# List pages padded ahead of time, y rows loaded two tiles at a time, and a memset behind every y scatter

## The reference

```python
x = x + xattn(layernorm(x), ctx, ctx, lens, Wq, Wk, Wv, Wo)   # keys past lens[b] are masked
u = layernorm(x)
s = softmax(u @ centroids.T + expert_biases)                  # 16 experts
topk_vals, topk_idx = top_k(s, 2)
routed = sum over the two of topk_vals * (u @ Wr[e].T + br[e])
shared = (u @ Ws[0].T + u @ Ws[1].T + bs[0] + bs[1]) / 2
x = x + u + routed + shared
```

## Time and profile before

| | us |
|---|---|
| Median of 3 runs (lowest, highest) | 261.77 (260.43, 262.01) |
| The profiled execution's own time | 261.29 |
| Its span in the profile | 259.4 |
| PE busy in the span | 219.6 (85%) |
| DVE busy | 152.5 (59%) |
| POOL busy | 106.3 (41%) |
| ACT busy | 95.1 (37%) |
| Mean granted TensorE clock, share of full | 0.953 |

### The profile page before, as it was taken

How to read it: one execution, slowest core, us unless ns; L and a number is a source line. 1 busy time by engine, 2 the same in 40 slices (tenths; PEclk the granted TensorE clock), 3 DMA queues, 4 the chain that set the end, 5 groups by cost and what they waited for, 6 DMA issues and landing times.

```text
span 259.4 us, 5036 instructions
## 1 busy us (share of the span) xinstructions
PE 219.6 (85%) x1530; PEld 184.8 (71%) x1530; DVE 152.5 (59%) x457; ACT 95.1 (37%) x241; POOL 106.3 (41%) x176
## 2 busy tenths in 40 slices
PE   7888999999999999999997943988669978576593
PEld 3767888888899998888875832867547757454482
DVE  1798778888888888888645930657503313140460
ACT  3114567566656666555442001222202213110022
POOL 1220222444444555444667200467566566574000
PEclk9999999999999999999999995999995999997689
DMA  6999990101011111100212693667455541200997
GB/s 170 361 247 373 426 414 16 43 20 44 20 44 41 43 41 44 42 22 27 79 39 71 159 206 100 201 197 221 137 169 163 172 130 36 90 17 9 332 382 248
DMA packets 20345, 36.30 MB, mean 140 GB/s; under 512 B 4059, under 2 KB 12765, under 8 KB 19936
## 3 DMA queue, kind: packets, MB, share of 16 engines
q1 hardware_dynamic: 13568, 22.50, 27.4%
q0 software_dynamic: 3792, 8.42, 9.2%
q10 hardware_dynamic: 2960, 5.07, 6.5%
HBM read 23.23 MB, written 14.71 MB: 146 GB/s over the span
## 4 chain that ended last, share of the span: by engine, by line
PE 67%; issue 9%; DMA 8%; DVE 4%; another core or an unknown queue 3%; SPq 3%; POOL 3%; ACT 1%; ACTq 1%; DVEq 0%; POOLq 0%
PE O L886 13%; PE T L808 7%; PE B L845 6%; PE B L953 5%; PE S L808 5%; PE A L808 4%; PE S L857 4%; PE B L1057 4%; PE T L1057 4%; PE A L1057 3%; DMA x<-in_x 3%; PE O L1057 3%; SPq L321 2%; PE S L1076 2%
## 5 line engine op out<-in xcount | busy, mean ns | idle before, releaser
L537 POOL DMA_INDIRECT lists<-urow,pos x32 | 32.8, 1024 | 41.6 <-PE S L857 34.0
L488 ACT ACTIVATE uTl<-S 128x256 f32<-128x256 f32 x47 | 17.0, 383 | 58.5 <-PE S L808 37.1
L415 ACT ACTIVATE pT<-T 128x512 f32<-128x512 f32 (+1 forms) x48 | 25.2, 526 | 30.4 <-PE T L808 28.7
L886 PEld LDWEIGHTS O<-vfront,pT 128*128 128x128 f32 x256 | 30.0, 192 | 0.1
L886 PE MATMUL O<-vfront,pT 128*128 128x34 f32 x256 | 29.9, 273 | 0.0
L665 DVE TENSOR_REDUCE rowmax<-S 128x16 f32<-128x1232 f32 x16 | 23.1, 1442 | 7.2 <-PE S L857 7.1
L568 POOL DMA_INDIRECT y<-yrow,padblock x16 | 15.8, 989 | 27.9 <-DVE yrow L786 20.7
L808 PE MATMUL T<-const,s_sb 128*128 128x128 f32 (+1 forms) x160 | 25.4, 273 | 2.0 <-DVE s_sb L680 1.2
L808 PEld LDWEIGHTS T<-const,s_sb 128*128 128x128 f32 (+1 forms) x160 | 19.1, 139 | 4.5 <-issue 2.7
L441 ACT ACTIVATE urow<-x,shift,rstds 128x256 f32<-128x256 f32 x32 | 19.1, 596 | 8.4 <-POOL shift L551 7.5
L680 DVE SCALAR_TENSOR_TENSOR s_sb<-S,rstds,scaledmax 128x1024 f32<-128x1024 f32 (+1 forms) x26 | 21.0, 850 | 0.0
(11 more groups left out here) (188 smaller groups left out, 432.7 us busy)
## 6 DMA issues: line engine op xcount, KB each, us to landing
padblock<-lists SPq DMA_DIRECT2D x32, 128.5 KB, 1.7
wr<-in_wrT SPq DMA_DIRECT2D x1, 4096.0 KB, 17.8
br<-in_br SPq DMA_DIRECT2D x1, 2048.0 KB, 21.9
wr<-y SPq DMA_DIRECT2D x8, 256.0 KB, 7.2
wr<-y ACTq DMA_DIRECT2D x8, 256.0 KB, 8.2
urow<-lists SPq DMA_DIRECT2D x15, 128.5 KB
xT<-in_xT SPq DMA_DIRECT2D x3, 512.0 KB, 7.7
x<-in_x SPq DMA_DIRECT2D x3, 512.0 KB, 8.0
```

What stands on the lines that cost most here:

```text
L415: nc.scalar.activation(pT[t % 2][0:rows, c0:c1, :], T[0:rows, 0:c1 - c0, :], ACT.Exp).then_inc(p_ready, 1)
L537: nc.gpsimd.indirect_dma_start(out=lists, out_offset=bass.IndirectOffsetOnAxis(ap=pos[:, t, c:c + 1], axis=0), in_=urow[t % NR][c][:, :], ...
L886: last = M(to, pT[t % 2][0:v.shape[0], c, :], v.rearrange("p h j -> p (h j)"), start=(c == 0), stop=(c == CH - 1), skip_group_check=True)
```

## The change

1. Padding. POOL's memset of padblock covers all 16 rows per partition instead of 4. SP fills the first three pages of every region at the start (filled), ahead of x and xT of tiles 8 to 15, which are now one load each (XGROUPS). Later pages are padded in the loop, three tiles ahead of any row that could reach them (REACH): seen becomes seen_runs, the tally eight times over (128 columns); PE multiplies it by one column of ones (count_runs), which gives each partition, an eighth of an expert, its expert's count; DVE rounds it to a page (reached, page), adds 4096 where the page is the same as a tile earlier (dropped), and so has the place in run_i; POOL writes 16 rows from each partition by an indirect DMA (pad_page), of which those past the bounds are dropped. pad_lists, padrow and the constant region go.
2. HANDOVER is 12, so the shared products of tiles 12 and 13 move behind the lists.
3. load_y takes two tiles, 512 KB; there are four loads on each queue.
4. POOL sets 256 columns of passed_x to zero behind every y scatter but the last.

```diff
-HANDOVER = 14
+HANDOVER = 12
+PARTS = P // EXPERTS
+RUN = P // PARTS
+REACH = 3
...
-        XGROUPS = [(0, 2), (2, 4), (4, 8), (8, 12), (12, 16)]
+        XGROUPS = [(0, 2), (2, 4), (4, 8), (8, 16)]
...
-            of = y_dram[b * SEQ * TOPK:(b + 1) * SEQ * TOPK, :].rearrange("(p t c) d -> t p c d", t=PER, c=TOPK)[t % PER]
-            eng.dma_start(ysum[:, t, :, :], of).then_inc(y_back[t], 16)
+            of = y_dram[b * SEQ * TOPK:(b + 1) * SEQ * TOPK, :].rearrange("(p t c) d -> p t c d", t=PER, c=TOPK)
+            eng.dma_start(ysum[:, t:t + 2, :, :], of[:, t % PER:t % PER + 2, :, :]).then_inc(y_back[t // 2], 16)
...
             sp.wait_ge(pool_set, 3)
-            sp.dma_start(lists[DUMMY:DUMMY + P, :], padblock[:, 0, :]).then_inc(padded, 16)
-            for g in (3, 4):
-                load_x(sp, g)
-                load_xT(sp, g)
+            sp.dma_start(lists[DUMMY:DUMMY + P, :], padblock[:, 0, :]).then_inc(filled, 16)
+            per_expert = lists[0:DUMMY, :].rearrange("(e n) w -> e n w", e=EXPERTS)
+            for page_of in range(REACH):
+                sp.dma_start(per_expert[:, page_of * P:(page_of + 1) * P, :].rearrange("e (b r) w -> e b (r w)", r=RUN),
+                             padblock[:, :, :].rearrange("p r w -> p (r w)")).then_inc(filled, 16)
+            load_x(sp, 3)
+            load_xT(sp, 3)
...
-            pad_lists(sp, mybir.EngineType.SP, 0, EXPERTS // 2)
-            sp.wait_ge(table_ready, 2)
+            sp.wait_ge(table_ready, 1)
...
-                    sp.wait_ge(padded, 16 + 16 * EXPERTS)
+                    sp.wait_ge(filled, 16 * (1 + REACH))
+                    for i in range(2):
+                        sp.wait_ge(padded[i], 16 * len(range(1 + i, TILES - REACH + 1, 2)))
...
-            pad_lists(act, mybir.EngineType.Activation, EXPERTS // 2, EXPERTS)
...
-            nc.gpsimd.memset(padblock[:, 0:PIECE, 0:D], 0.0)
+            nc.gpsimd.memset(padblock[:, :, 0:D], 0.0)
...
+                if t == 0:
+                    pool.wait_ge(filled, 16 * (1 + REACH))
+                if t >= REACH:
+                    pool.wait_ge(padded[(t - REACH) % 2], 16 * ((t - REACH) // 2 + 1))
...
+            def pad_page(t):
+
+                pool.wait_ge(run_ready, t)
+                nc.gpsimd.indirect_dma_start(
+                    out=runs, out_offset=bass.IndirectOffsetOnAxis(ap=run_i[:, t:t + 1], axis=0),
+                    in_=padblock[:, :, :].rearrange("p r w -> p (r w)"), in_offset=None,
+                    bounds_check=DUMMY // RUN - 1, oob_is_err=False).then_inc(padded[(t - 1) % 2], 16)
+
             for s in range(TILES + 3):
...
                 if is_tile(s - 3) and s != TILES:
                     scatter_rows(s - 3, s)
+                if 1 <= s - 3 <= TILES - REACH:
+                    pad_page(s - 3)
...
+                if k < LISTS - 1:
+                    if k >= 2:
+                        pool.wait_ge(paused, k - 1)
+                    nc.gpsimd.memset(passed_x[:, k % 2, :], 0.0).then_inc(paused, 1)
...
+                    opens = 1 <= t <= TILES - REACH
+                    if opens:
+                        V.tensor_scalar(reached[:, :], run_bank(t), REACH * P - FRONT - 0.5, 1.0 / RUN, ALU.add, ALU.mult
+                                        ).then_inc(reached_ready, 1)
...
-                        V.tensor_tensor(seen[:, :], seen[:, :], chosen[:, :], ALU.add)
+                        V.tensor_tensor(seen_runs[:, :, :], seen_runs[:, :, :],
+                                        chosen[:, :].unsqueeze(2).to_broadcast([P, EXPERTS, PARTS]), ALU.add)
...
+                    if opens:
+                        dve.wait_ge(reached_ready, t)
+                        link(V.tensor_scalar(page[:, t:t + 1], reached[:, :], EIGHTS, EIGHTS, ALU.add, ALU.subtract))
+                        link(V.tensor_scalar(dropped[:, :], page[:, t - 1:t], page[:, t:t + 1], BEYOND, ALU.is_equal, ALU.mult))
+                        V.scalar_tensor_tensor(out=run_i[:, t:t + 1], in0=page[:, t:t + 1], scalar=cst("run"), in1=dropped[:, :],
+                                               op0=ALU.add, op1=ALU.add).then_inc(run_ready, 1)
...
+            def count_runs(t):
+
+                if 1 <= t <= TILES - REACH:
+                    M(run_bank(t), seen_runs[:, :, :].rearrange("p e b -> p (e b)"), ones16[:, 0:1], start=True, stop=True)
...
-                pe.wait_ge(y_back[t], 16)
+                pe.wait_ge(y_back[t // 2], 16)
```

More of the change, by code:

```diff
@@ L182, in build @@
         start_i = sb("start_i", [LISTS, 1], i32)
-        padrow = sb("padrow", [1, EXPERTS], i32)
-        RUN, PIECE, NL, NY, NU = 16, 4, 24, 16, 4
+        reached = sb("reached", [P, 1])
+        page = sb("page", [P, TILES])
+        dropped = sb("dropped", [P, 1])
+        run_i = sb("run_i", [P, TILES], i32)
+        NL, NY, NU = 24, 16, 4
         padblock = sb("padblock", [P, RUN, ROW])
@@ L252, in build @@
         shifted_ready = sem("shifted_ready")
-        padded = sem("padded")
+        filled, padded, run_ready = sem("filled"), [sem(f"padded{i}") for i in range(2)], sem("run_ready")
+        reached_ready = sem("reached_ready")
+        paused = sem("paused")
         l_arrived = [sem(f"l_arrived{j}") for j in range(NL)]
```

52 lines of the change are left out of this document (25 added, 27 removed).

## The result

The changed kernel took 263.6 us in the median of 20 runs (260.7 to 268.2), the kernel before 260.8 us on the same chip. The ratio is 1.0067, with a 95% interval of 1.0042 to 1.0092: slower by 0.7%, within what I had called no change. The ratio leaves out executions more than 1.5% above the fastest of their kernel, seven of the twenty and the profiled one among them, and the medians of all lie 1.1% apart. I had said 264.9 us and 45% for slower by over 1%. The sum came out near the mark by luck: all that stands ahead of the list stage cost 5.8 us where I had said a gain of 3.2, and the list stage gained 2.4 us where I had said a loss of 5.3.

A forecast was written before the change was run, and what follows sets the result against it. TensorE was taken to bound the loop, with VectorE's add without slack, and GpSimd's scatters the lists. Minus 3.2, plus 5.3, plus 1.0 gave 264.4 us, and 0.5 for the median 264.9; range 255.0 to 269.5.

The forecast's parts named there:

- (f): List stage, memset behind 46 y scatters: interval 1.67 us against 1.29, stage 76.8 instead of 71.5, plus 5.3 us.
- (c): GpSimd in the loop, 13 more page DMAs: tile 12's page costs 1.26 us on the path, tile 13's nothing.
- (d): Start: padding memset grows to 3.8 us, then 6.4 MB of fill ahead of x and xT; cost nothing.
- (e): Before the lists: padding DMAs go, TensorE stays warm, first load to first y scatter 5.6 us; that scatter 3.2 earlier.
- (a): VectorE's page operations in the loop: 0.68 us ahead of each add, 6.8 us over ten periods.
- (b): TensorE in the loop: one more weight load and one-column product, 0.10 us per tile, hidden in its wait; nothing.
- the first rival: List stage: memset runs largely within the launch gap, interval near 1.45 us, stage 66.7, total 254.8; chance 0.22.
- (g): Two-tile y loads at the end: first result 1.3 us late, two more VectorE operations after the last arrival; plus 1.0 us.
- the other rivals: Free page operations, 259.4, chance 0.10; page scatters several times dearer, 270, 0.09; TensorE at 1.2 GHz in lists, 269.5, 0.07.

## Why the prediction came out as it did

It said slower by a little, and 264.9 us is near; both are luck. In its sum the loop lost 8.1 us, the shorter path to the first scatter of y gave back 11.3, and the slowing came from the list stage, plus 5.3. Measured, everything up to the first scatter of y cost 5.8 us (1.3 + 8.8 + 5.0 - 9.2), and the list stage gained 2.4. Both signs were wrong, and the errors cancelled. The largest step that failed is (f), which had the memset cost the stage 5.3 us; the others are (c), (d) and (e), each with a term put at nothing or too low, and the size of (a). Step by step:

- **(a), VectorE in the loop, was right in its mechanism, and too small.** Predicted 0.68 us ahead of each add and a period of 8.0; measured 0.66 and 8.0. Moving three operations took it back to 7.42, which shows the cause. What I missed is a period at a lower clock: 1.6 us more for one of 9.6, in four of the five profiles whose loop ran at 8.0 us. Of the fifteen that ran at 7.34 or 7.42, three have a period at a mean clock of 0.80 or 0.81, and only among the last two, where no queries follow. That TensorE's longer waits bring it about is a guess; no run varied them alone. And it is eleven periods, not ten. Together 8.8 instead of 6.8.
- **(b), TensorE's count of runs, was not tested by itself.** The period's 0.66 us are accounted for by VectorE's operations, which leaves nothing for it; of the 0.08 us that stay when three of them are moved it may be a part.
- **(c) failed at the page of tile 13.** The page of tile 12 costs its 1.3 us as said. That of tile 13 "stands behind that norm, among scatters that wait for pos anyway": I priced its issue and not its landing. The scatters of tile 15 wait for that page, which is issued at 151.16 and lands at 158.0. The wait is 4.0 us and stands on the path; this term was put at nothing. Padding four tiles ahead took 1.2 of it off, and then pos was late.
- **(d) failed at the start.** The fill is hidden, as said, but the memset ahead of it is not. I had reckoned that it ends 2.8 us later (it ended at 16.0 and not at 17.6) and looked only at the fill. It kept VectorE's scaledmax from running (2.17 us instead of 0.70), and the loop began 1.3 us late. The trace of before had shown it in small: scaledmax ran from 14.14 for 0.70 us and ended as the memset of the earlier trace rows did.
- **(e) failed in its warm TensorE.** From the last row scatter to the first scatter of y: -9.2, predicted -11.3. The first list load goes out 2.9 us after the last row scatter began, as I had it; from there to the first scatter of y it was 7.7 us as before, and not 5.6. TensorE had run out of shared products 2.6 us before the first row came, as (c) had put off the last row scatter, and its granted clock over this stretch was 0.78 (0.60 before). The profiles of the other kernels with padded pages bear this out: seven with a granted clock of 1.00 there took 6.7 to 7.4 us, and three at 0.56 to 0.78 took 7.7 to 7.9. So a warm TensorE seems to be worth up to 1 us here, and the other 1.1 of my 2.1 were not to be had.
- **(f), the memset, was the largest error.** The term was mis-sized at 1.67 us an interval; it measured 1.46. I had put 0.07 us ahead of the memset, 0.22 behind it and 1.09 for the scatter; the memset starts where the scatter ends, the gap behind it is 0.17, and the scatter keeps its 0.97. Beside VectorE's work the memset itself took 0.33 us in the median instead of 0.31, so the contention that I weighed there is small. At 46 x 0.21 = 9.7 us less the first rival was right about this stage: it gave 1.45 and said that the stage shrinks. It came to 69.1 us and not 66.7, since shorter stalls remain. The total was not its 254.8, because (a), (c), (d) and (e) were together 9 us too low. I had given this rival 22%.
- **(g)** Predicted +1.0, measured -0.1 in the spans, and 0.9998 for the loads alone. The 8 us that I worked out from the fit in the Trainium skill (DMA: Bandwidth & Descriptors, Anatomy of one DMA) and did not believe are not there, and the loads cost nothing either.

Of the other rivals none came. The page operations did extend the period. A page scatter's issue takes 1.00 us like the others; what its longer rows lengthen is the landing. TensorE's clock over the list stage was 0.98.

And one premise failed that no step names: that the stalls of 2.6 us belong to the kernel. They belong to the kernel on a certain chip. The sign of (f) turns on that: -2.4 us in the profiles here, +8.0 on chip N, where the whole change costs 4.9%.

## What to carry to other kernels

Put what a change adds to an engine behind the operation that the bounding engine waits for, not just where its inputs are ready; moving the same three operations behind it gave 2.6%. Of an added transfer count the landing as well as the issue, and ask who waits for it last, at the end of the loop. Idle time that is bridged by spacing should be measured on more than one chip before the spacing is kept.

## What the runs showed of the hardware

- **A stall that some chips have.** On the first chip and on A, B and C the scatters of y come back to back at 1.29 us, and roughly every 10 us one or two intervals last 2.0 to 3.7 us, in which the other engines start next to nothing (read in four of them in the kernel before). On chip N the same scatters run through. An interval of 1.46 us makes the stalls shorter and rarer, one of 1.69 removes them. What holds the engines was not settled: held register loads are excluded by their durations, and that any instruction between the scatters would break the stalls is excluded by the run with 16 columns.
- **A memset of GpSimd can hold an operation of VectorE.** scaledmax, a tensor_scalar of 16 columns that otherwise takes 0.23 us, took 2.17 when it started 1.4 us into GpSimd's memset of 4096 columns. It ended at 16.13, 0.11 us behind the memset's end. The tensor_reduce rowmax, which ran beside the same memset, took its usual 1.44. The Trainium skill (SBUF — State Buffer, Who interferes with whom) says that VectorE in a two-port mode, which a tensor_scalar can enter and a tensor_reduce cannot, contends with GpSimd for a shared port pair; whoever issues first has the pair for the whole instruction, and the other is fully blocked. The trace agrees in both.
- **A memset behind an indirect DMA on GpSimd starts at once,** and the launch of the next DMA shrinks from 0.30 to 0.17 us behind it. 16 columns add nothing to the interval, 256 add 0.17 us and 512 add 0.40.
- **A register load costs the engine that issues it 0.37 us in a row of them** (TensorE, 47 started within 17.2 us), and in the list stage 16 at a time opened gaps of 3 to 4 us.
